# A graph network on one core: the adjacency comes with its axes swapped, r and z get a second PSUM bank, and three engines take their work in new orders

## What is computed

```python
# layer 0, on h = relu(layernorm(x))
x_conv = relu(bn2(conv17(relu(bn1(conv1(h))))) + h)       # along the nodes
s = h @ w_se.T + b_se                                     # 3 columns
A = exp(-dist(s, s)) * adj                                # 256x256 per graph
x_nmp = A @ relu(h @ w_msg.T + b_msg)
gi = concat([x_conv, x_nmp]) @ w_ih.T + b_ih              # 512 -> 768
gh = h @ w_hh.T + b_hh                                    # 256 -> 768
r, z = sigmoid(gi_r + gh_r), sigmoid(gi_z + gh_z)
n = tanh(gi_n + r * gh_n)
x = x + (1 - z) * n + z * h
# layer 1, on h = relu(layernorm(x))
x = x + relu(h @ weight[:256] + (adj @ h) @ weight[256:] + bias)
```

## Time and profile before

| what | value |
|---|---|
| median of three runs | 2043.64 us |
| the profiled execution, its own time | 2046.88 us |
| its span, first to last instruction | 2045.1 us |
| mean granted TensorE clock | 0.980 |
| busy: PE, PE's weight loads, DVE | 93%, 70%, 73% |
| busy: ACT, POOL | 39%, 19% |
| share of the 16 DMA engines, queue of SyncE | 32.7% |

### The profile page before, as it was taken

One profiled execution on the slowest core, in us unless ns is written; L12 is line 12 of the kernel. 1 busy time (PEld: TensorE's weight loads), 2 busy tenths in 40 slices (PEclk: granted clock), 3 DMA queues, 4 the chain that ended last, 5 costly groups with the idle time before them and its releaser, 6 DMA issues.

```text
span 2045.1 us, 37541 instructions
## 1 busy us (share of the span) xinstructions
PE 1910.9 (93%) x13020; PEld 1440.8 (70%) x13020; DVE 1486.3 (73%) x3296; ACT 798.1 (39%) x1480; POOL 378.7 (19%) x554
## 2 busy tenths in 40 slices
PE   2877989999975999999999999999999999999997
PEld 2666767764434777777777777777777777877775
DVE  3977878852234777877777778777777787777775
ACT  3854445544224333333333333333333333333332
POOL 1021111100011222121221222212212222122120
PEclk9989999999987999999999999999999999999998
DMA  3076565656234222222322223223222232232220
GB/s 109 1 283 232 184 226 196 198 212 257 98 139 146 68 85 68 93 77 72 98 68 85 85 68 96 73 73 97 68 90 80 68 100 70 75 95 68 91 79 16
DMA packets 162857, 224.40 MB, mean 110 GB/s; under 512 B 15863, under 2 KB 112878, under 8 KB 162030
## 3 DMA queue, kind: packets, MB, share of 16 engines
q1 hardware_dynamic: 159550, 223.35, 32.7%
q10 hardware_dynamic: 3248, 0.27, 0.1%
HBM read 133.39 MB, written 90.18 MB: 109 GB/s over the span
## 4 chain that ended last, share of the span: by engine, by line
PE 63%; DVE 3%; ACT 2%; issue 0%; DMA 0%; ACTq 0%; POOLq 0%; POOL 0%; DVEq 0%
PE ps_rz L1291 26%; PE ps_n L1291 13%; PE ps_l L1291 13%; PE ps_b L1291 9%; DVE nmp L1397 2%; ACT nmp L1392 2%; PE ps_adj L1317 1%; PE ps_d L1300 1%; DMA rows<-spectra 0%; ACTq L1213 0%; PE ps_s L1251 0%; PE ps_d L1515 0%; DVE out_sum L1567 0%; DVE out_sb L1571 0%; DVE update L1480 0%
## 5 line engine op out<-in xcount | busy, mean ns | idle before, releaser
L1446 ACT ACTIVATE tanh_rz<-sum_rz,w_scale 128x512 f32<-128x512 f32 x128 | 92.7, 724 | 473.8 <-DVE sum_rz L1437 473.8
L882 PE MATMUL m_ps<-big 128*128 128x512 f16 (+1 forms) x1152 | 268.5, 376 | 4.1 <-DVE ysb L792 2.1
L1291 PE MATMUL ps_rz<-w_ih,nmp 128*128 128x512 f32 x768 | 206.6, 404 | 11.4 <-DVE nmp L1397 11.3
L1471 POOL TENSOR_TENSOR x_new<-xin,new 128x256 f32<-128x256 f32 x128 | 93.5, 731 | 663.5 <-ACT new L1464 663.5
L1291 PE MATMUL ps_rz<-w_ih,conv_t 128*128 128x512 f32 x768 | 209.1, 407 | 0.0
L882 PEld LDWEIGHTS m_ps<-big 128*128 128x128 f16 x1152 | 112.4, 98 | 108.5 <-DVE ysb L792 3.6
L1291 PE MATMUL ps_rz<-w_hh,ht 128*128 128x512 f16 x768 | 186.8, 379 | 0.9 <-DVE sum_n L1440 0.9
L1291 PE MATMUL ps_l<-w_l,h2t 128*128 128x512 f16 x768 | 179.4, 384 | 1.4 <-DVE h2t L1527 1.4
L1291 PEld LDWEIGHTS ps_rz<-w_ih,nmp 128*128 128x128 f32 x768 | 134.7, 188 | 51.1 <-DVE nmp L1397 26.6
L792 DVE SCALAR_TENSOR_TENSOR ysb<-m_ps,ysb 128x512 f16<-128x512 f32 x96 | 66.1, 689 | 118.5 <-ACT ysb L718 118.5
L1291 PEld LDWEIGHTS ps_rz<-w_ih,conv_t 128*128 128x128 f32 x768 | 134.8, 189 | 23.8
(11 more groups left out here) (219 smaller groups left out, 3814.7 us busy)
## 6 DMA issues: line engine op xcount, KB each, us to landing
xin<-in_x SPq DMA_DIRECT2D x128, 256.0 KB, 2.9
spectra<-ysb SPq DMA_DIRECT2D x96, 256.0 KB, 2.0
rows<-spectra SPq DMA_DIRECT2D x64, 384.0 KB, 3.5
x_normed<-xhat SPq DMA_DIRECT2D x64, 256.0 KB, 3.3
h_turned<-ht SPq DMA_DIRECT2D x64, 256.0 KB, 2.4
adj_in<-in_adj SPq DMA_DIRECT2D x64, 256.0 KB, 3.7
ht<-h_turned SPq DMA_DIRECT2D x64, 256.0 KB, 3.3
xhat<-x_normed SPq DMA_DIRECT2D x64, 256.0 KB, 2.9
```

The costliest lines, as they stand in the source:

```text
L882: last = pe.matmul(dest, x_, w_, start=n == 0, stop=n == 11, skip_group_check=True)
L1291: last = pe.matmul(dest, stationary(dl), moving(wl), start=start and n == 0, stop=stop and n == 2, **kw)
L1446: act.activation(tanh_rz[:, i, :], sum_rz[:, i, :], ACT.Tanh, scale=w["scale"][:, 4:5]).then_inc(S["rz_tanh"], 1)
L1471: pool.tensor_tensor(x_new[:, i, :], xin[:, p, i, :], new[:, i, :], ALU.add).then_inc(S["x_new_done"], 1)
```

## The change

- The host hands over adj with the last two axes swapped, and `turn_adj` with its bank and its semaphore goes. `attention`, `adj_split_high` and `adj_split_low` read the loaded tile adj_in in SBUF where they read ps_adj in PSUM, and wait for the load.
- ps_rz becomes two banks, one for each tile. `first_h` waits for the sums of r and z of the graph before alone; the wait for ps_n's sum of the tile before stands behind the r and z matmuls.
- `gates_first` is cut into `first_h`, `first_conv_rz` and `first_conv_n`, and the queues get new orders:

The diff, without the parts that only carry out these orders:

```diff
-    adj_d = adj.rearrange("g (t p) m -> g p t m", p=P)
+    adj_d = adj.rearrange("g (m p) n -> g p m n", p=P)
...
-        ps_adj = ps("ps_adj")
-        ps_rz = ps("ps_rz")
+        ps_rz = [ps(f"ps_rz{i}") for i in range(H)]
...
         def load_rows(sp, t, p):
...
-            before(sp, "adj_turned", t, 1, 2)
+            before(sp, "att_done", t, 1, 2)
+            before(sp, "adj_low", t, 1, 2)
             sp.dma_start(adj_in[:, p, :, :], adj_d[t]).then_inc(adj_loaded[p], 16)
...
-        def turn_adj(pe, t, p):
-            arrived(pe, adj_loaded, t, p)
-            before(pe, "att_done", t)
-            before(pe, "adj_low", t)
-            for m in range(H):
-                for i in range(H):
-                    last = pe.transpose(ps_adj[:, m * N + i * P:m * N + i * P + P],
-                                        adj_in[:, p, i, m * P:m * P + P], ident[:, :])
-            last.then_inc(S["adj_turned"], 1)
-
         def adj_split_high(act, t, p):
-            ready(act, "adj_turned", t)
+            arrived(act, adj_loaded, t, p)
             before(act, "out_done", t, H, 2)
-            act.activation(adj_t[:, p, 0, :, :].rearrange("p h n -> p (h n)"), ps_adj[:, :],
-                           ACT.Copy).then_inc(S["adj_high"], 1)
+            act.activation(adj_t[:, p, 0, :, :], adj_in[:, p, :, :], ACT.Copy).then_inc(S["adj_high"], 1)
...
         def adj_split_low(dve, t, p):
...
-            dve.tensor_tensor(adj_t[:, p, 1, :, :].rearrange("p h n -> p (h n)"), ps_adj[:, :],
-                              adj_t[:, p, 0, :, :].rearrange("p h n -> p (h n)").bitcast(F32),
+            dve.tensor_tensor(adj_t[:, p, 1, :, :], adj_in[:, p, :, :], adj_t[:, p, 0, :, :].bitcast(F32),
                               ALU.subtract).then_inc(S["adj_low"], 1)
...
         def attention(dve, t, p):
             ready(dve, "exp_done", t)
+            arrived(dve, adj_loaded, t, p)
...
-            dve.tensor_tensor(att[:, :, :].rearrange("p h n -> p (h n)"),
-                              ps_adj[:, :], expd[:, :, :].rearrange("p h n -> p (h n)"),
-                              ALU.mult).then_inc(S["att_done"], 1)
+            dve.tensor_tensor(att[:, :, :], adj_in[:, p, :, :], expd[:, :, :], ALU.mult).then_inc(S["att_done"], 1)
...
-        def gates_first(pe, t, p, i):
-            ready(pe, "rz_added", t, i, H)
+        def first_h(pe, t, p, i):
+            before(pe, "rz_added", t, H)
+            for kh in range(H):
+                three(pe, ps_rz[i][:, :], lambda s: ht[:, p, s, kh, i * P:i * P + P],
+                      lambda s: w["hh"][:, s, kh, 0:2 * D], kh == 0, False)
             ready(pe, "n_added", t, i, H)
...
+        def first_conv_rz(pe, t, p, i):
             if i == 0:
                 ready(pe, "conv_low", t)
...
+        def first_conv_n(pe, t, p, i):
...
-        value = np.ascontiguousarray(value)
+        value = np.ascontiguousarray(value.transpose(0, 2, 1) if name == "adj" else value)
```

More of the change, by code:

```diff
@@ L1197, in gates @@
         names = ("msg_done msg_added "
-                 "msg_high msg_low adj_turned adj_high adj_low dist_done exp_done att_done att_high att_low "
+                 "msg_high msg_low adj_high adj_low dist_done exp_done att_done att_high att_low "
                  "nmp_done nmp_high nmp_low conv_high conv_low rz_done n_done rz_added n_added rz_tanh "
@@ L1399, in weighted_low @@
                               ALU.subtract).then_inc(S["nmp_low"], 1)
-        def gates_first(pe, t, p, i):
-            ready(pe, "rz_added", t, i, H)
+        def first_h(pe, t, p, i):
[3 more added lines that the diff above has]
+                      lambda s: w["hh"][:, s, kh, 0:2 * D], kh == 0, False)
             ready(pe, "n_added", t, i, H)
-            for kh in range(H):
-                three(pe, ps_rz[:, :], lambda s: ht[:, p, s, kh, i * P:i * P + P],
-                      lambda s: w["hh"][:, s, kh, 0:2 * D], kh == 0, False)
             for kh in range(H):
@@ L1414, in gates_first @@
             for kh in range(H):
-                three(pe, ps_rz[:, :], lambda s: conv_t[:, p, s, kh, i * P:i * P + P],
+                three(pe, ps_rz[i][:, :], lambda s: conv_t[:, p, s, kh, i * P:i * P + P],
                       lambda s: w["ih"][:, s, kh, 0:2 * D], False, False)
+        def first_conv_n(pe, t, p, i):
             for kh in range(H):
@@ L1425, in gates_second @@
             for kh in range(H):
-                last = three(pe, ps_rz[:, :], lambda s: nmp[:, s, kh, i * P:i * P + P],
+                last = three(pe, ps_rz[i][:, :], lambda s: nmp[:, s, kh, i * P:i * P + P],
                              lambda s: w["ih"][:, s, 2 + kh, 0:2 * D], False, kh == H - 1)
@@ L1436, in gate_sums @@
             before(dve, "rz_tanh", t, H)
-            dve.tensor_tensor(sum_rz[:, i, :], ps_rz[:, :], w["bias_rz"][:, :], ALU.add).then_inc(S["rz_added"], 1)
+            dve.tensor_tensor(sum_rz[:, i, :], ps_rz[i][:, :], w["bias_rz"][:, :], ALU.add).then_inc(S["rz_added"], 1)
             ready(dve, "n_done", t, i + 1, H)
@@ L1634, in slot @@
                     if cur:
-                        adj_split_high(act, t, p)
                         exponential(act, t, p)
@@ L1641, in slot @@
                         messages_high(act, t, p)
+                        adj_split_high(act, t, p)
                         weighted_high(act, t, p)
+                    if nxt:
+                        conv_read(act, t + 1, 1 - p)
                     if prev:
                         h2_split_high(act, t - 1, 1 - p)
-                    if nxt:
-                        conv_read(act, t + 1, 1 - p)
                     if cur:
@@ L1649, in slot @@
                         new_tanh(act, t, p, 0)
+                    if nxt:
+                        conv_split_high(act, t + 1, 1 - p)
                     if prev:
                         passed_high(act, t - 1, 1 - p)
-                    if nxt:
-                        conv_split_high(act, t + 1, 1 - p)
                 slots(act, slot)
@@ L1669, in slot @@
                         messages_add(dve, t, p)
-                    if prev:
-                        x1_rows(dve, t - 1, 1 - p, 1)
-                    if cur:
                         att_split_low(dve, t, p)
@@ L1675, in slot @@
                     if prev:
+                        x1_rows(dve, t - 1, 1 - p, 1)
                         x1_stats(dve, t - 1, 1 - p, 1)
@@ L1678, in slot @@
                         adj_split_low(dve, t, p)
+                        weighted_low(dve, t, p)
                     if prev:
@@ L1681, in slot @@
                     if cur:
-                        weighted_low(dve, t, p)
+                        gate_sums(dve, t, p, 0)
                     if prev:
@@ L1685, in slot @@
                     if cur:
-                        gate_sums(dve, t, p, 0)
                         gate_new(dve, t, p, 0)
+                        x1_rows(dve, t, p, 0)
+                        x1_stats(dve, t, p, 0)
                     if prev:
                         passed_low(dve, t - 1, 1 - p)
-                    if cur:
-                        x1_rows(dve, t, p, 0)
-                        x1_stats(dve, t, p, 0)
                     if nxt:
@@ L1706, in slot @@
                     if cur:
-                        turn_adj(pe, t, p)
                         distances(pe, t, p)
                         messages(pe, t, p)
-                        gates_first(pe, t, p, 0)
+                        first_h(pe, t, p, 0)
+                        first_conv_rz(pe, t, p, 0)
                         weighted(pe, t, p)
+                        first_conv_n(pe, t, p, 0)
                     if nxt:
                         inverse(pe, t + 1, 1 - p)
+                    if cur:
+                        gates_second(pe, t, p, 0)
                     if prev:
@@ L1716, in slot @@
                     if cur:
-                        gates_second(pe, t, p, 0)
+                        first_h(pe, t, p, 1)
                     if prev:
@@ L1720, in slot @@
                     if cur:
-                        gates_first(pe, t, p, 1)
+                        first_conv_rz(pe, t, p, 1)
+                        first_conv_n(pe, t, p, 1)
                     if prev:
```

## The result

The changed kernel takes 1997.76 us (median of 4 runs, 1996.95 to 2000.75) against 2043.36 for the kernel before (4 runs): ratio 0.9777, 95% interval 0.9761 to 0.9794. Forecast were 1999 us and a range of 1985 to 2020. The profiled execution took 1998.04 us, with a span of 1996.2 us; the mean granted clock is 0.980 in both.

A forecast was written before the change was run, and what follows sets the result against it. PE's queue bounds the kernel: 20.61 us of kept work plus a 0.20 us stall give a 20.81 us slot, 0.70 less; over 64 slots 44.8 us off 2043.64, rounded to 1999 us, range 1985 to 2020 us.

The forecast's parts named there:

- The bound: A slot of 21.51 us lasts as long as PE's queue; PE is busy 198.43 of 200 us.
- The kept work: PE's groups in a slot, from `distances` to `gates_second(1)`, that the change keeps, claimed to sum to 20.61 us.
- Part 1: Removing the four adjacency transposes takes all 0.44 us out of PE's slot and costs nothing.
- The rival by which only the transposes pay: DVE or ACT is late somewhere, stalls stay at 0.46 us a slot; 28.2 us less, 2015.5 us; chance 15%.
- Part 2: PE's stall before `gates_second(0)` falls from 0.46 to 0.20 us: 0.09 us too early plus 0.11 for a restart.
- the restart: Extra 0.11 us that PE's group `gates_second(0)` costs after a wait, against 1.40 us without one.
- Parts 3 and 4: DVE ends `adj_split_low` 0.05 us before nmp's low part must start; the earlier `weighted` has 0.2 us of cover.
- Part 5: `attention` and the two splits read SBUF instead of PSUM; bounds -0.03 and +0.03 us each, taken as nothing.
- Part 6: The second r and z bank gains nothing in a full slot; a loss only if 0.85 us go.
- Part 7: `turn2` comes later; `layer1` keeps 0.3 us of slack on h's low part, where it was over 1 us.
- The rule: DVE instructions with two SBUF inputs and SBUF-reading GpSimd ones share a port; the later one blocks fully.
- its rival: GpSimd's two small operations get in before `adj_split_low` and hold it up; slot 21.7 us, 2056 us; chance 7%.

The follow-up runs named there:

- the halves: Changed kernel with one bank for r and z, the freed bank taking the first half of `weighted`'s result, nmp split in two halves: 1988.24 us, ratio 0.9725.
- the swap alone: Kernel before with the adjacency handed over swapped and the transposes gone, all orders and the single r and z bank as before: 2050.1 us, ratio 1.0035.
- the run with the memsets: Changed kernel with two memsets on VectorE right before `adj_split_low`, so that GpSimd's two small operations start first: 2018.19 us, ratio 0.9874.
- the orders alone: Changed kernel with the transposes put back and one bank for r and z: 2024.88 us, ratio 0.9910.

## Why the prediction was right

- *The bound.* Right: every run is its PE queue plus what PE waits for, and 64 times the change of the mean slot gives the change of the time within 2 us in all ten.
- *The kept work, 20.61 us.* Right as a sum (20.80 less 0.09 and 0.11), in part by luck. The terms were taken to be the same in the new order. `layer1` takes 2.40 us to the next start and not 2.60, h's products of tile 1 take 1.96 and not 1.87, the convolution's 2.30 and not 2.18: they cancel to 0.01 us.
- *Part 1, the transposes' 0.44 us.* Right in the sum (0.41 us in the pair with and without them), but only under the new orders. With the old ones their removal runs into the messages' low part 0.3 us further on and into h2hat, and brings a loss of 7 to 8 us. The rival by which only the transposes pay, 2015 us, supposed that the stalls still come to 0.46 us in the new order; the trace has 0.20.
- *Part 2, the stall from 0.46 to 0.20 us.* Right: from `weighted` to `gates_second(0)` 3.09 us of chain against 3.00 of work. Shown by the n products put back, which make the stall what 2.29 us of cover leave, and by the halves, which take it away. Its 0.11 us for the restart was mis-sized: 0.05 go with the wait, and 0.06 are there behind `inverse` without one.
- *Parts 3 and 4, VectorE's order.* Right in its direction: `x1_rows` in its old place costs 60 us. The tightest place had 0.26 us rather than 0.05 between `adj_split_low`'s end and the low part of nmp, since `adj_split_low` starts at 6.31 and not at 6.47. The step that was wrong here is that the chain until `messages_high` runs as before: it starts 0.16 us earlier, as exp is out of its way. VectorE's 3.11 us from the low parts to `adj_split_low` were right (3.15). `weighted` has 0.37 us of cover for the same reason, and not 0.2. The error was on the safe side. ScalarE's new order, norm2 behind `weighted_low` and `turn2` behind `gates_second(0)` were not tried one by one.
- *Part 5, operands from SBUF at nothing.* VectorE's own operations kept their 0.66 and 0.69 us. ScalarE's `adj_split_high`, which the part did not price, went from 0.58 to 0.62 us, where nothing waits for it. The cost is on GpSimd: 0.35 us for its addition. In the changed kernel it is covered by what the trace shows (no run tries it by itself), since `norm2` now stands behind `weighted_low`, and `turn2` starts 2.4 us after `norm2` does. In the swap alone it is not covered and costs 9 to 10.5 us. The prediction named the stretch, from 0.20 to some 0.5 us, and the cover.
- *Part 6, the second bank.* Right: nothing.
- *Part 7, `layer1`'s cover.* Right: h2t's low part ends at 1218.64 us in the slot shown, and no wait of PE on it is listed in a full slot.
- *The rule and its rival.* GpSimd came second, as forecast, and waited. That its power would have held VectorE for 0.70 us, had it come first, is refuted: in the run with the memsets `adj_split_low` starts 0.21 us into it and takes 0.63 us. GpSimd's 256-column x_new does hold up VectorE's diff. The Trainium skill (SBUF — State Buffer, SBUF: two separate sides) states that whichever of two such operations starts first gets the shared pair of ports for the whole instruction. For the 128x2 power the measured 0.63 us differs from this, and the measurement decides. So the rival's 2056 us could not have come from the power, which was nearly all of it; the 0.20 us of the addition ahead of it were not tried.

## What to carry to other kernels

When one engine's queue is full, removing work from it pays only if what it runs into next is also earlier: list for each wait of that queue the cover in front of it, take the removed time off every cover, and move independent groups of work to where the cover falls short. An operand moved from PSUM to SBUF cost VectorE nothing here, but can hold up a short GpSimd operation that starts just after it; look who waits for that one. Measure an order and a removal apart: here the removal alone lost 7 to 8 us, the orders alone won 18, and together they won 46. A group's distance to the next start is not its own alone: after a change of order, take it again, as three groups moved by 0.09 to 0.20 us here and cancelled by luck.

## What the runs showed of the hardware

- GpSimd's 128x2 addition takes 0.20 us alone and 0.55 us when it starts 0.16 us after a 128x512 VectorE operation with two SBUF inputs, in all 61 slots looked at. Where that operation is moved away it takes 0.20 us again (58 and 59 slots of two runs).
- GpSimd's 128x2 power, 0.70 us long, does not delay such an operation that starts 0.21 us into it (0.63 us, the same in all 60 slots), while x_new with 256 columns stretches one of 256 columns from 0.42 to 0.83 us.
- With its input in SBUF instead of PSUM, ScalarE's 128x512 `adj_split_high` takes 619 ns on average instead of 576; VectorE's `adj_split_low` takes 658 in both.
- A PE group of six 512-column matmuls takes 1.39 to 1.40 us to the next start behind `neighbours`, 1.46 behind `inverse` without a wait, and 1.49 to 1.51 where it starts 0.09 to 0.79 us late: within this range the price of a wait beyond its length is the same.
